# attention0: head pairs on the two row halves of TensorE, stacks through DRAM, projections and layer norms in pieces

## Chip, cores and metric

The program runs on one core of one Trainium2 chip. Its time is the device time of one execution in microseconds. A core has TensorE (PE, matmuls; PEld its weight loads), VectorE (DVE), ScalarE (ACT), GpSimd (POOL) and SyncE (SP, which here only issues DMAs). Operands lie in SBUF, matmul results in eight PSUM banks of 128 x 512 float32.

## What is computed

Two layers over x of shape 16 x 512 x 128. In each layer the normalised x goes through an attention and, beside it, through a feed-forward part whose SiLU gates the attention's result. The change touches only the attention of the first layer, with 16 heads of width 8:

```python
Q = jax.nn.relu(x @ Wq + bq)
K = jax.nn.relu(x @ Wk + bk)
V = jax.nn.relu(x @ Wv + bv)
...
scores = jnp.einsum('bqhd,bkhd->bhqk', Qh, Kh) / np.sqrt(dh)
scores = jnp.where(key_mask[:, None, None, :] == 0, NEG, scores)
scores = jnp.where(tril[None, None, :, :] == 0, NEG, scores)
attn = jax.nn.softmax(scores, axis=-1)
attn = attn * query_mask[:, None, :, None]
out = jnp.einsum('bhqk,bkhd->bqhd', attn, Vh).reshape(B, T, U)
out = out + x
```

and then a layer norm with gamma and beta. What follows it in the kernel (times the gate, plus x, and the layer norm of the next layer) is done in the same function.

## The kernel before

The program runs one stage after the other: exact layer norm, `ffn`, `attention0`, `attention1`, `experts`. `attention0` takes the span from 386 to 1429 us. It works batch by batch (16 batches of 512 tokens), each batch in two units of 8 heads, so 32 units; two batches (four units) are one turn of the loop, with the first and the last turn written out. Each engine has its own order, written by hand; semaphores tie them together.

**Operands.** A head is only 8 wide, and float32 accuracy is wanted from bf16 matmuls. So q and k are each split into three bf16 parts (ACT writes the first, `split` on POOL the two others), and six part products are stacked on the rows of one matmul: 48 rows, a mask row and, for the second pass, three rows with the parts of the row maximum. The stacks `QS` and `KS` (four buffers each, one for a unit) are filled by SP with copies of 64 KB from SBUF to SBUF, 6 for QS and 6 for KS per unit, and one mask row (`stack`, L730; `mask_row`, L735). Because the rows used are 0 to 95 or 0 to 98, a matmul of these takes the whole height of the array, and a stack holds the 8 heads of a unit.

**Two passes.** The first pass computes the scores only for the row maximum: `max_bank` (L1082, L1084) fills a PSUM bank pair `pMax` with queries on the partitions (four query blocks of width 128 to 512, since it is causal), adds `far` (a very negative triangle) with a full 128 x 128 matmul per head, and DVE takes the maximum (`maxima`, L948). `m_split` on DVE splits the 32 maxima of a unit in three parts, `turn_m` (L1136) turns them on PE, ACT copies them to SBUF (`m_evac`) and SP puts them on rows 96 to 98 of QS (`m_rows`, L740). The second pass, `score_bank` (L1095, and `add_far`, L624 and L627), computes the scores with the keys on the partitions, the maximum already subtracted; ACT takes the exponential of each bank of 512 into `PT` (`exps`, L887, five banks for two heads, two buffers `pST`). `weigh` (L1123) multiplies by the values in float32, four heads at a time in four column strips of the array; the denominators come from a column of V. ACT copies the result (`o_evac`, L892), PE turns it back (`turn_o`, L1130), and DVE divides (`o_normal`).

**Order.** In unit u, `both` interleaves the score banks of u with the max banks of u+1 (16 of them, the first ones before anything else, done by the third pair). `turn_m(u+1)` stands in the fourth pair; then the product with the values; then unit u+1 begins with `wait_ge(m_put, ...)`. In even units the next batch is prepared: transpose of x, q and k projections, and at the end the values. SP issues, in an even unit, 12 copies for QS and 6 for KS, then `m_rows`, then 6 more. All small PE results (x, q, k, v, the turned output and maxima) go through one bank, `pM`, one after another. The layer norms (`normalise`, `normalise_x1`) and the evacuation of the values (`v_evac`, L965 to L973) stand on DVE as whole blocks at the end of a unit.

Of the kernel before, what the change touches and what calls it, by code (L numbers as in the profile page):

```python
# [629 lines left out]
def attention0(nc, NB, XN, G, KM, ident, identb, far, x, Wq, bq, Wk, bk, Wv, bv, gamma, beta, x1_d, mask_d):  # L630

# [3 lines left out]
    PARTS_Q = (0, 0, 0, 1, 1, 2)  # L642
    PARTS_K = (0, 1, 2, 0, 1, 0)
    MASK, MROW = 64, 96
    VC = DH + 1
    PER_D, PER_G = 112, 20
    STACK = 7 * 16
    with ExitStack() as c:
# [7 lines left out]
        rows = sb("rows", [P, 3, P])  # L656
        xst = sb("xn_staged", [P, TOK])
# [4 lines left out]
        QS = [sb(f"QS{i}", [P, UH, TOK], BF16) for i in range(4)]  # L662
        KS = [sb(f"KS{i}", [P, UH, TOK], BF16) for i in range(4)]
        V = [sb(f"V{i}", [P, TB, HEADS * VC + 32 - VC]) for i in range(2)]
        vtmp = sb("vtmp", [P, TB, P])
        PT = [sb(f"PT{i}", [P, 5, TOK]) for i in range(4)]
        MX = sb("max", [P, UH, TB])
        mrest = sb("mrest", [P, UH * TB])
        mp = sb("mparts", [P, 3, UH * TB], BF16)
        mT = sb("mT", [UH * TB, 3, P], BF16)  # L670
        OT = sb("OT", [P, TOK])
        den = sb("den", [P, TB, 4])
# [6 lines left out]
        pST = [ps(f"pST{i}", [P, TOK]) for i in range(2)]  # L679
# [5 lines left out]
        zeroed, ones_set, v_set = sem("k_zeroed"), sem("k_ones_set"), sem("v_set")  # L685
        q_zeroed, q_ones_set = sem("q_zeroed"), sem("q_ones_set")
# [8 lines left out]
        q_stacked, k_stacked = [sem(f"q_stacked{i}") for i in range(2)], [sem(f"k_stacked{i}") for i in range(2)]  # L695
# [8 lines left out]
        loads = 3 + 2 * 2 * DH + 3  # L704

        @block.sync
        def _(sp):
# [12 lines left out]
            sp.wait_ge(mask_made, 3)  # L720
            sp.dma_start(mask_d, part[0:NT, 1, 0, 0:P]).then_inc(mask_stored, 16)
            sp.wait_ge(mask_stored, 16)

# [4 lines left out]
            def stack(i0, half, n, S, order, stacked):  # L728
                for at, k in enumerate(order):
                    sp.dma_start(S[i0 + half][DH * at:DH * at + DH, :, :],  # L730
                                 part[64 * half:64 * half + 64, n, k, :]).then_inc(stacked[half], 16)

            def mask_row(b, i0, half):
# [3 lines left out]
            def m_rows(u, i):  # L737
                mT_in.wait(sp, u)
                for k in range(3):
                    sp.dma_start(QS[i][MROW + k:MROW + k + 1, :, :], mT[:, k, :]).then_inc(m_put, 16)  # L740

# [189 lines left out]
        def _(v):  # L931
# [83 lines left out]
            for p in range(4):  # L1015
                maxima(0, p)
# [1088 lines left out]
```

## Times and profile before

| | us |
|---|---|
| median of 3 runs | 3515.97 (3511.75 to 3518.88) |
| profiled execution, device time | 3512.28 |
| its span, first to last instruction | 3510.6 |
| attention0 in it | 386 to 1429 |
| attention1 in it | 1429 to about 2900 |
| mean granted TensorE clock, whole span | 0.935 |

The page divides the span into 40 slices of 87.8 us; attention0 fills slices 5 to 17, and attention1 the next ones up to slice 33. Digits such as PE 7, DVE 6 or 7 and ACT 4 or 5 there say that no engine is busy all the time in attention0, while in attention1 PE stands at 9. The granted clock is 1.0 at 2.4 GHz and 0.5 at 1.2 GHz; a mean between the two is a mixture in time.

### The profile page before, as it was taken

Reading aid. Unit: us, or ns where it says so; the run is one execution under the profiler, and the core shown is the slowest. Engines: PE = TensorE matmul, PEld = TensorE weight load, DVE = VectorE, ACT = ScalarE, POOL = GpSimd, SP = SyncE. Lnnn points to the kernel's source line nnn. Section 1 sums busy time; section 2 is a strip of 40 time slices with the busy share of each in tenths; the row PEclk is TensorE's granted clock in tenths of the full one; section 3 lists DMA queues with packets and bytes.
Section 4 is the critical chain, followed back from the end, with each engine's and each line's share of the span. In section 5 each row is a group of like instructions: output and inputs, shape, how many; then the busy total and the mean of one; then the engine's idle time right before and its main releaser. Section 6 shows DMA issues by size and latency. Waiting matters only on the chain. (4 is left out here: it accounts for less than half of the span.)

```text
span 3510.6 us, 66700 instructions
## 1 busy us (share of the span) xinstructions
PE 2817.1 (80%) x21313; PEld 1947.4 (55%) x21313; DVE 2341.5 (67%) x5836; ACT 1521.8 (43%) x2623; POOL 1262.9 (36%) x1384
## 2 busy tenths in 40 slices
PE   0046367777777788499999999999999987999999
PEld 0024134444444444366666666666666656888888
DVE  8978657777776777466666666666666645555555
ACT  3434234454444455254555545555555532232232
POOL 4546602121211211155555555555555550000000
PEclk9986579998989899699999999999999998999999
DMA  1000123222221312101111111111111112010100
GB/s 48 0 6 0 25 30 47 39 44 35 41 45 36 51 35 32 37 28 35 34 34 34 34 34 34 34 34 34 34 34 34 32 35 64 24 36 24 34 26 24
DMA packets 152527, 116.24 MB, mean 33 GB/s; under 512 B 35506, under 2 KB 127155, under 8 KB 152372
## 3 DMA queue, kind: packets, MB, share of 16 engines
q1 hardware_dynamic: 152372, 114.25, 14.2%
q8 instruction: 87, 1.43, 0.2%
q14 instruction: 68, 0.56, 0.1%
HBM read 60.96 MB, written 17.32 MB: 22 GB/s over the span
## 5 line engine op out<-in xcount | busy, mean ns | idle before, releaser
L1539 DVE CUSTOM_DVE_ANT_0 a_scored<-a_pMax,a_causal 128x128 bf16<-128x128 f32 (+3 forms) x1024 | 449.7, 485 | 444.0 <-PE a_pMax L1663 444.0
L948 DVE TENSOR_REDUCE a_max<-a_pMax 128x2 f32<-128x256 f32 (+3 forms) x512 | 406.8, 822 | 209.3 <-PE a_pMax L1084 198.4
L887 ACT ACTIVATE a_PT<-a_pST 128x512 f32<-128x512 f32 x640 | 370.6, 597 | 403.3 <-PE a_pST L624 268.4
L1456 ACT ACTIVATE a_PT<-a_pST 128x1024 f32<-128x1024 f32 (+1 forms) x384 | 338.8, 882 | 361.2 <-PE a_pST L1653 349.8
L1082 PE MATMUL a_pMax<-a_KS,a_QS 96*128 96x128 bf16 (+3 forms) x1024 | 283.8, 329 | 203.3 <-DMA a_QS<-a_mT 134.6
L1405 POOL TENSOR_SCALAR_AFFINE_SELECT a_PT<-a_PT 128x256 f32<-128x256 f32 x512 | 203.0, 409 | 603.5 <-ACT a_PT L1456 573.0
L1942 ACT ACTIVATE m_silu<-m_pG 128x512 f32<-128x512 f32 x256 | 153.3, 599 | 410.2 <-PE m_pG L2034 410.2
L1671 PE MATMUL a_pO<-a_PT,a_V 128*64 128x512 f32 (+3 forms) x2048 | 307.3, 443 | 0.7 <-POOL a_PT L1405 0.7
L1082 PEld LDWEIGHTS a_pMax<-a_KS,a_QS 96*128 96x128 bf16 x1024 | 106.8, 105 | 309.4 <-issue 197.9
L1095 PE MATMUL a_pST<-a_QS,a_KS 99*128 99x512 bf16 (+3 forms) x1024 | 256.8, 315 | 16.4 <-ACT a_PT L887 14.4
L2042 PEld LDWEIGHTS m_pY<-m_w,m_hT 128*128 128x128 f32 x2048 | 248.0, 191 | 9.9
L815 POOL TENSOR_TENSOR a_rest<-a_qk,a_parts 128x512 f32<-128x512 f32 x32 | 37.0, 1155 | 593.9 <-ACT a_parts L880 593.7
L1989 DVE TENSOR_TENSOR m_hT<-m_pU,m_silu 128x512 f32<-128x512 f32 x256 | 177.0, 691 | 108.9 <-PE m_pU L2034 90.6
L2042 PE MATMUL m_pY<-m_w,m_hT 128*128 128x128 f32 x2048 | 248.8, 275 | 0.0
L1423 POOL TENSOR_TENSOR a_SM<-a_PT 128x768 f32<-128x768 f32 x128 | 235.0, 1836 | 10.6
L1671 PEld LDWEIGHTS a_pO<-a_PT,a_V 128*64 128x64 f32 x2048 | 136.6, 137 | 164.5 <-issue 145.3
L1910 POOL TENSOR_TENSOR m_out<-m_silu_acc,m_y 128x512 f32<-128x512 f32 x16 | 20.3, 1270 | 561.5 <-ACT m_silu_acc L1934 561.5
L1084 PE MATMUL a_pMax<-far,identb 128*128 128x128 bf16 x1024 | 221.9, 235 | 0.0
L2002 DVE SCALAR_TENSOR_TENSOR m_acc<-m_pY,m_cw,m_acc 128x128 f32<-128x128 f32 x448 | 126.3, 344 | 126.8 <-PE m_pY L2042 126.8
L1646 PE MATMUL a_pST<-a_q_high,a_k_high 64*128 64x512 f32 (+3 forms) x1024 | 198.9, 385 | 4.0 <-ACT a_PT L1456 4.0
L1653 PE MATMUL a_pST<-a_max_rows,a_ones_rows 64*128 64x512 f32 (+3 forms) x1024 | 151.8, 333 | 50.5 <-DMA a_max_rows<-a_mT 50.5
L1663 PE MATMUL a_pMax<-a_k_high,a_q_high 64*128 64x128 f32 (+3 forms) x1024 | 166.8, 363 | 8.0 <-DVE a_max L1539 6.6
(282 smaller groups left out, 6861.7 us busy)
## 6 DMA issues: line engine op xcount, KB each, us to landing
a_rden<-inverse_sums_dram SPq DMA_DIRECT2D x256, 128.0 KB, 2.9
a_QS<-a_parts SPq DMA_DIRECT2D x192, 64.0 KB
a_KS<-a_parts SPq DMA_DIRECT2D x192, 64.0 KB
a_xn_staged<-xn SPq DMA_DIRECT2D x32, 256.0 KB, 2.4
a_max_rows<-a_mT SPq DMA_DIRECT2D x512, 2.0 KB
ln_x<-in_L_attn_x SPq DMA_DIRECT2D x8, 512.0 KB, 7.2
a_x<-in_L_attn_x SPq DMA_DIRECT2D x16, 256.0 KB, 3.0
x_dram<-a_att SPq DMA_DIRECT2D x16, 256.0 KB, 3.8
```

Of the source, the lines that this page charges most:

```text
L887: a.activation(PT[p][:, k], pST[(5 * p + k) % 2][:], ACT.Exp, scale=SCALE).then_inc(exped.sem, 1)
L948: v.tensor_reduce(MX[:, 2 * p:2 * p + 2, j], pMax[j % 2][:, :, 0:(j + 1) * P], AX.X, ALU.max, negate=True).then_inc(maxed.sem, 1)
L1082: pe.matmul(pMax[j % 2][:, hh, 0:(j + 1) * P], QS[i][0:MROW, h, j * P:(j + 1) * P], KS[i][0:MROW, h, 0:(j + 1) * P], start=True, stop=False)
L1084: mm = pe.matmul(pMax[j % 2][:, hh, j * P:(j + 1) * P], identb[:], far[:], start=False, stop=True)
L1095: pe.matmul(bank[:, at:at + TOK - kb * P], KS[i][0:MROW + 3, h, kb * P:(kb + 1) * P], QS[i][0:MROW + 3, h, kb * P:TOK], start=(at == 0), s ...
L1405: g.affine_select(out=blocks, in_=blocks, compare_op=ALU.is_ge, fill=0.0, base=0, pattern=[[0, 2], [1, P]], channel_multiplier=-1).then_in ...
L1423: step.then(g.tensor_tensor(S[:, :, P:TOK], T[:, :, P:TOK], T[:, :, AT[1]:AT[1] + TOK - P], ALU.add))
L1456: a.activation(PT[s.q % 2][:, :, k * TOK:k * TOK + w], pST[:, :, 0:w], ACT.Exp, scale=SCALE).then_inc(exped.sem, 1)
L1539: last = v.tensor_tensor_reduce(scored[:, cc, at:at + w], pMax[:, cc, at:at + w], causal[:, TOK - w:], -1.0, 3e38, ALU.add, ALU.min, MX[pa ...
L1646: pe.matmul(pST[:, cc, at:at + w], K[i][rows, keys], Q[i][rows, queries], start=(n == 0 and at == 0), stop=False)
L1671: mm = pe.matmul(pO[DH * cc:DH * cc + DH, kb * P:TOK], V[pair // 2 % 2][:, kb, head:head + DH], PT[pair % 2][:, cc, AT[kb]:AT[kb] + TOK - ...
L2042: mm = pe.matmul(pY[e % 2][:, t], HT[HC * (e % 2) + k][:, t * P:(t + 1) * P], W2[:, e, k], start=(k == 0), stop=(k == HC - 1))
```

## The change

Only `attention0` is changed (and two DRAM tensors for it are declared).

- A head pair is now a head of the first eight and the same one of the second eight. The first lies on rows 0 to 63 of the array, the second on rows 64 to 127: 48 rows of part products, a row of ones against the mask row, three rows for the maximum. QS and KS hold a whole batch each (two buffers instead of four), a unit is four head pairs.
- Max pass: three rounds per pair (`max_round`) with widths 512, 128 and 384, 256 for each half; score pass: three rounds (`score_round`) of 512, 384 and 128, 256 for each half, all in one `pST` of two banks, where the next round waits for the exponential of the one before. `far` is still added with full 128 x 128 matmuls, one per half and round. Exponentials are 1024, 1024 and 512 wide.
- The max rounds run six pairs ahead of the scores (`LEAD`), so the maxima of unit u+1 are complete after the second pair of unit u.
- SP writes the parts of q and of k to DRAM (3 DMAs each and the mask row), waits for them, and loads the stacks from there: two DMAs of 448 KB for KS and two of 384 KB for QS, for the batch after this one. PE waits for them in an even unit before the third pair (`batch_stacked`).
- q and k of the batch after next are projected in odd units; the values of the next batch in even units, in two pieces, with the bias as a one-row matmul; their ReLU and copy is one ACT instruction instead of nine of DVE.
- The product with the values and both layer norms are cut in pieces which stand between score rounds (PE) or maxima (DVE).

```diff
+    PAIRS, NS, NM, LEAD = 4, 3, 3, 6
+    AT = (0, TOK, 2 * TOK, TOK + 3 * P)
+    WIDTH = (TOK, TOK, 2 * P)
+    ROUNDS = (((0, 0),), ((0, 1), (3 * P, 3)), ((0, 2),))
+    MAXB = (((3, 0),), ((0, 0), (2, P)), ((1, 0),))
...
+        pST = ps("pST", [P, 2, TOK])
...
+            def lead(self, p, last):
+                ahead = 1 if p < 2 else 2
+                if last and self.s + ahead > 3:
+                    return None
+                return self.u + ahead, (self.s + ahead) % 4, (p + 2) % PAIRS
...
+            def put_parts(dst, n, groups, put):
+                for at, count, k, parts in groups:
+                    src = part[:, n, k:k + 1, :].to_broadcast([P, count, TOK]) if parts == 1 else part[:, n, k:k + count, :]
+                    sp.dma_start(dst[at:at + count].rearrange("a s d h t -> (s d h) a t"), src).then_inc(put, 16)
...
+            def stack(b, parity, last_score=None):
+                sp.wait_ge(q_put, PUT_Q * (b + 1))
+                sp.sem_inc(puts_seen, 1)
+                sp.wait_ge(k_put, PUT_K * (b + 1))
+                sp.sem_inc(puts_seen, 1)
+                if last_score is not None:
+                    st_ready.wait(sp, last_score)
+                for half in range(2):
+                    sp.dma_start(KS[parity][key_rows(half), :, :], ks_d[:, half].rearrange("a d h t -> a d (h t)")).then_inc(k_stacked, 16)
+                for half in range(2):
+                    sp.dma_start(QS[parity][part_rows(half), :, :], qs_d[:, half].rearrange("a d h t -> a d (h t)")).then_inc(q_stacked, 16)
...
+                    n = Unit(i, s, first, last)
+                    u, b = n.u, n.b
+                    if not n.odd:
+                        if n.values:
+                            stack(b + 1, 1 - n.parity, NS * PAIRS * u - 1)
+                        if not (last and s == 0) and not (last and s == 2):
+                            stage(b + 2)
+                        if not n.no_before:
+                            load_x(b - 1)
+                    elif not n.no_before:
+                        store_x1(b - 1, 1 - n.parity)
+                    if n.prepare:
+                        put_q(b + 2)
+                    if not n.end:
+                        m_rows(u + 1, (s + 1) % 4 // 2, (s + 1) % 2)
+                    if n.prepare:
+                        put_k(b + 2)
...
+            def exp(u, p, k):
+                if k == 0:
+                st_ready.wait(a, NS * (PAIRS * u + p) + k)
+                at, w = k * TOK, WIDTH[k]
+                a.activation(PT[p][:, :, at:at + w], pST[:, :, 0:w], ACT.Exp, scale=SCALE).then_inc(exped.sem, 1)
...
+                    exp(u, 0, 2)
+                    exp(u, 1, 0)
+                    if n.prepare:
+                        q_evac(b + 2)
+                    exp(u, 1, 1)
+                    if not n.start:
...
+                    exp(u, 3, 0)
                     o_evac(2 * u)
+                    if n.prepare:
+                        k_evac(b + 2)
+                    exp(u, 3, 1)
+                    exp(u, 3, 2)
...
+            def values(b, ts=(0, 1, 2, 3)):
+                for t in ts:
+                    into = pM[:, t * P:(t + 1) * P]
+                    pe.matmul(into, XT[:, t * P:(t + 1) * P], wv[:], start=True, stop=False)
+                    mm = pe.matmul(into, one[0:1, :], rows[0:1, 0, :], start=False, stop=True)
+                if ts[-1] == TB - 1:
+                    mm.then_inc(v_ready.sem, 1)
+
+            def max_round(u, par, pair, p, m):
+                n = NM * (PAIRS * u + p) + m
+                bank = pMax[(NM * p + m) % 2]
+                maxed.wait(pe, n - 2)
+                for k, (j, at) in enumerate(MAXB[m]):
+                    w = (j + 1) * P
+                    for half in range(2):
+                        pe.matmul(bank[:, half, at:at + w], QS[par][masked_rows(half), pair, j * P:(j + 1) * P],
+                                  KS[par][masked_rows(half), pair, 0:w], start=(k == 0), stop=False)
+                for half in range(2):
+                    mm = add_far(pe, bank[:, half], [at + j * P for j, at in MAXB[m]], identb, far)
                 mm.then_inc(max_ready.sem, 1)
...
+            def score_round(u, par, pair, p, k):
+                exped.wait(pe, NS * (PAIRS * u + p) + k - 1)
+                for at, kb in ROUNDS[k]:
+                    for half in range(2):
+                        rows = split_rows(half)
+                        pe.matmul(pST[:, half, at:at + TOK - kb * P], KS[par][rows, pair, kb * P:(kb + 1) * P],
+                                  QS[par][rows, pair, kb * P:TOK], start=(at == 0), stop=False)
+                for half in range(2):
+                    mm = add_far(pe, pST[:, half], [at for at, _ in ROUNDS[k]], far, identb)
+                mm.then_inc(st_ready.sem, 1)
...
+                    def scores(p, k):
+                        score_round(u, par, PAIRS * group + p, p, k)
+                        lead(p, k)
+
+                    def weigh_before(kbs):
+                        if not n.start:
+                            weigh(u - 1, 1, 1 - group, par if n.odd else 1 - par, kbs)
+
+                    pe.wait_ge(m_put, M_PUT * (u + 1))
+                    scores(0, 0)
+                    weigh_before((0,))
+                    scores(0, 1)
+                    weigh_before((1,) if n.prepare else (1, 2, 3))
+                    if n.prepare:
+                        o_in.wait(pe, 2 * u - 2)
+                        turn_x(b + 2)
+                    scores(0, 2)
+                    scores(1, 0)
+                    if n.prepare:
+                        weigh_before((2, 3))
+                        project(b + 2, wq, q_ready)
+                    elif not n.start:
+                        o_in.wait(pe, 2 * u - 2)
+                    if n.start:
+                        mT_in.wait(pe, 0)
+                    if n.values:
+                        values(b + 1, (0, 1))
+                    scores(1, 1)
+                    if n.values:
+                        values(b + 1, (2, 3))
+                    scores(1, 2)
+                    if not n.odd and n.lead(2, last) is not None:
+                        batch_stacked(b + 1)
+                    scores(2, 0)
+                    if n.prepare:
+                        q_in.wait(pe, b + 2)
+                    if n.values:
+                        v_in.wait(pe, b + 1)
+                    if not n.start:
                         turn_o(2 * u - 1)
...
+                    weigh(u, 0, group, par, (0,))
+                    scores(2, 1)
+                    weigh(u, 0, group, par, (1,))
+                    scores(2, 2)
+                    if not n.end:
+                        o_in.wait(pe, 2 * u - 1)
+                        turn_m(u + 1)
+                    scores(3, 0)
+                    weigh(u, 0, group, par, (2, 3))
+                    if n.prepare:
                         mT_in.wait(pe, u + 1)
-                        values(b + 1)
+                        project(b + 2, wk, k_ready)
+                    scores(3, 1)
+                    scores(3, 2)
+                    if n.prepare:
+                        k_in.wait(pe, b + 2)
+                    elif n.end:
+                        o_in.wait(pe, 2 * u - 1)
+                    else:
+                        mT_in.wait(pe, u + 1)
+                    turn_o(2 * u)
```

On PE, a pair of the middle of a unit before: scores of unit u (pST) between maxima of unit u+1 (pMax), each max matmul with its own `far`.

```order
L1082 MATMUL a0_pMax1<-a0_KS2,a0_QS2 128x256
L1084 MATMUL a0_pMax1<-far,identb 128x128
L1082 MATMUL a0_pMax1<-a0_KS2,a0_QS2 128x256
L1084 MATMUL a0_pMax1<-far,identb 128x128
L1095 MATMUL a0_pST0<-a0_QS1,a0_KS1 128x384
L1095 MATMUL a0_pST0<-a0_QS1,a0_KS1 128x128
L627 MATMUL a0_pST0<-identb,far 128x2x128
L1082 MATMUL a0_pMax0<-a0_KS2,a0_QS2 128x384
```

The same place after the change, on PE, behind the projection of q (L1150); the printed name of a stack gives no row half, "x2" are the two halves.

```order
L1150 MATMUL a0_pM<-a0_xT,a0_wq 128x512 [waits a0_xT_in]
L1178 MATMUL a0_pST<-a0_QS0,a0_KS0 128x384 [waits a0_exped]
L1178 MATMUL a0_pST<-a0_QS0,a0_KS0 128x384
L1178 MATMUL a0_pST<-a0_QS0,a0_KS0 128x128 x2
L627 MATMUL a0_pST<-identb,far 128x2x128 x2
L1167 MATMUL a0_pMax0<-a0_KS1,a0_QS1 128x128 [waits a0_maxed]
L1167 MATMUL a0_pMax0<-a0_KS1,a0_QS1 128x128
L1167 MATMUL a0_pMax0<-a0_KS1,a0_QS1 128x384 x2
L627 MATMUL a0_pMax0<-far,identb 128x2x128 x2
L1178 MATMUL a0_pST<-a0_QS0,a0_KS0 128x256 [waits a0_exped]
```

What moved: matmuls on row halves and full-height `far` matmuls now alternate in blocks, twice for each score and max round, and every score round carries a wait for the exponential of the one before.

On SP, a turn before, from the preparation of a batch to the rows of the maxima.

```order
L730 DMA a_QS<-a_parts 8x8x512 [waits a0_st_ready,a0_q_parts]
L730 DMA a_QS<-a_parts 8x8x512 x11
L730 DMA a_KS<-a_parts 8x8x512 [waits a0_k_parts]
L730 DMA a_KS<-a_parts 8x8x512 x5
L735 DMA a_KS<-mask_dram 1x8x512
L740 DMA a_QS<-a_mT 1x32x128 [waits a0_mT_in]
```

And on SP after the change, from the end of an odd unit into the even one.

```order
L746 DMA k_parts_dram<-a_parts 128x3x512 [waits a0_k_parts]
L746 DMA k_parts_dram<-a_parts 128x2x512
L746 DMA k_parts_dram<-a_parts 128x512
L760 DMA k_parts_dram<-mask_dram 2x8x512
L770 DMA a_KS<-k_parts_dram 56x1x4096 [waits a0_q_put,a0_k_put,a0_st_ready]
L770 DMA a_KS<-k_parts_dram 56x1x4096
L772 DMA a_QS<-q_parts_dram 48x1x4096 x2
L741 DMA a_xn_staged<-xn 128x512 [waits a0_x_turned]
```

What moved: 24 copies of 64 KB within SBUF became 7 writes to DRAM and 4 loads from it, and the loads stand behind a wait for the writes.

## Rows read from the trace of the kernel before

**Rows 1.** Windows, the steady stretch: us, busy by engine (x instructions), PEclk, DMA share, GB/s
```profile
520.00:1400.00 880.00, 676.31 (x5839) 392.13 (x5835) 645.56 (x1655) 425.13 (x751) 171.62 (x144) 0.91 0.25 41
```

**Rows 2.** Who waited for whom in that stretch: us in total, times, longest
```profile
PE a_pMax L1082 <- DMA a_QS<-a_mT: 124.3, 29, 8.4
```

**Rows 3.** PE: one transpose group per unit; a row of the timeline, first and last start
```profile
482.01 0.33 PE L1136 MATMUL a_pM<-identb,a_mparts 128*32 128x128 bf16 x3 [0.34 <-DVEq L960]
...
L1136 PE MATMUL a_pM<-identb,a_mparts x96: 216/219/314, 451.4 to 1386.7; 128*32 128x128 bf16 x96
```

**Rows 4.** Timeline of PE, start us and length us, attention0 at an undisturbed place
```profile
1292.88 0.38 PE L1095 MATMUL a_pST<-a_QS,a_KS 99*128 99x512 bf16 x1
1293.10 0.22 PE L624 MATMUL a_pST<-identb,far 128*128 128x128 bf16 x1
1293.16 0.33 PE L1082 MATMUL a_pMax<-a_KS,a_QS 96*128 96x384 bf16 x1
...
1298.09 0.60 PE L1130 MATMUL a_pM<-ident,a_OT 128*128 128x128 f32 x4
1298.53 0.22 PE L1082 MATMUL a_pMax<-a_KS,a_QS 96*128 96x128 bf16 x1
```

**Rows 5.** Timeline of PE around one product with the values
```profile
1290.24 2.36 PE L1123 MATMUL a_pO<-a_PT,a_V 128*32 128x512 f32 x32
1292.53 0.28 PE L1082 MATMUL a_pMax<-a_KS,a_QS 96*128 96x256 bf16 x1
```

**Rows 6.** Timeline of PE in attention1: row-half pairs and their neighbours
```profile
1727.06 0.28 PE L1701 MATMUL a_pD<-a_wvT_high,a_xT_low 128*128 128x256 f32 x1
1727.27 0.50 PE L1646 MATMUL a_pST<-a_q_high,a_k_high 64*128 64x512 f32 x2
1727.61 0.39 PE L1646 MATMUL a_pST<-a_q_low,a_k_high 64*128 64x512 f32 x2
...
1728.07 0.40 PE L1653 MATMUL a_pST<-a_max_rows,a_ones_rows 64*128 64x512 f32 x2
1728.30 0.45 PE L1663 MATMUL a_pMax<-a_k_high,a_q_high 64*128 64x128 f32 x4
1728.68 2.38 PE L1671 MATMUL a_pO<-a_PT,a_V 128*64 128x512 f32 x16
```

**Rows 7.** Timeline of ACT in attention1, the two widths of exp
```profile
1724.67 0.60 ACT L1456 ACTIVATE a_PT<-a_pST 128x512 f32<-128x512 f32 x1
...
1728.51 1.02 ACT L1456 ACTIVATE a_PT<-a_pST 128x1024 f32<-128x1024 f32 x1 [0.55 <-PE a_pST L1653]
```

**Rows 8.** Groups by form in 520 to 1400: xcount, busy us, mean ns, idle before
```profile
L971 DVE TENSOR_SCALAR a_V<-a_vtmp,key_mask 128x128 f32<-128x128 f32 x56 | 58.4, 1042 | 8.3 <-DVE a_V L973 2.8 <-DVE a_vtmp L965 2.5
...
L892 ACT COPY a_OT<-a_pO 128x512 f32<-128x512 f32 x60 | 35.1, 585 | 84.4 <-PE a_pO L1123 84.4
L815 POOL TENSOR_TENSOR a_rest<-a_qk,a_parts 128x512 f32<-128x512 f32 x28 | 32.4, 1156 | 547.3 <-ACT a_parts L880 547.3
...
L880 ACT ACTIVATE a_parts<-a_pM,a_bqk 128x512 bf16<-128x512 f32 x28 | 19.3, 689 | 0.0
```

**Rows 9.** Timeline of SP: twelve of the stack copies
```profile
1321.44 7.88 SPq L730 DMA_DIRECT2D a_QS<-a_parts  x12
```

**Rows 10.** Windows: after a long wait; stack copies; the experts' weight loads
```profile
1284.00:1290.00 6.00, 6.00 (x36) 4.16 (x37) 3.69 (x10) 2.01 (x4) 0.08 (x1) 0.59 0.33 64
1322.00:1330.00 8.00, 6.29 (x51) 3.88 (x50) 7.42 (x13) 5.17 (x10) 3.42 (x3) 1.00 0.48 69
2904.00:2916.00 12.00, 0.00 (x0) 0.00 (x0) 10.85 (x18) 3.39 (x3) 0.18 (x6) 0.50 0.95 290
```

**Rows 11.** DMA issues of the run: xcount, KB each, median us to landing
```profile
x_dram<-a_att SPq DMA_DIRECT2D x16, 256.0 KB, 3.8
...
a_QS<-a_mT SPq DMA_DIRECT2D x96, 8.0 KB, 2.6
```

**Rows 12.** Timeline of PE: the first instruction of the main loop
```profile
462.56 0.27 PE L1082 MATMUL a_pMax<-a_KS,a_QS 96*128 96x128 bf16 x1 [10.66 <-DMA a_KS<-mask_dram]
```

More of the change, by code:

```diff
@@ L726, in stage @@
                 sp.dma_start(xst[:].rearrange("p (t d) -> p t d", t=TB), XN[:, bass.ds(b * TB, TB), :]).then_inc(staged, 16)
[L728 to L733, printed above, removed]
-                row = mask_d[bass.ds(b * TB, TB), :].rearrange("(o a t) p -> o a (t p)", o=1, a=1)
-                sp.dma_start(KS[i0 + half][MASK:MASK + 1, :, :], row.to_broadcast([1, UH, TOK])).then_inc(k_stacked[half], 16)
@@ L842, in residual @@
                 g.sem_inc(x1_made.sem, 1)
+            step = Steps(g, pool)
+            for b in range(2):
+                split(step, b, 0, q_in, q_parts)
+                split(step, b, 1, k_in, k_parts)
+            before = step.n
+            tail = [None]
             def turn(i, first, last):
@@ L1024, in turn @@
                 if not first:
[L1025 removed]
+                    step.base = step.base - FIRST_LESS_D
                 for s in range(4):
[L1027 to L1033 removed]
@@ L1045, in turn, with lead @@
-                    if s % 2 == 0 and not (last and s == 2):
-                        v_evac(step, b + 1, 1 - par)
-                    if s % 2 == 1 and not (first and s == 1):
-                        normalise_x1(step, b - 1, 1 - par)
+                    n = Unit(i, s, first, last)
+                    u, b = n.u, n.b
+                    before_a = (b, 0, n.parity) if n.odd else (b - 1, 1, 1 - n.parity)
+                    def lead(p, m):
+                        target = n.lead(p, last)
+                        if target is not None:
+                            maxima(target[0], target[2], m)
@@ new lines, in layer_norm @@
+                    def layer_norm(piece, odd):
+                        if n.odd == odd and not n.no_before:
+                            (normalise_x1 if odd else normalise)(step, b - 1, 1 - n.parity, piece)
+                    lead(0, 0)
+                    if not n.start:
+                        o_normal(step, 2 * u - 2, before_a[0], before_a[1], 0, before_a[2])
+                    lead(0, 1)
+                    lead(0, 2)
+                    layer_norm(0, True)
+                    lead(1, 0)
@@ L1201, in next_m @@
-                    def next_m():
-                        if more:
-                            if first and s == 0:
-                                k_in.wait(pe, b + 1)
-                            else:
-                                o_in.wait(pe, 2 * u - 1)
-                            turn_m(u + 1)
-                    pe.wait_ge(m_put, 48 * (u + 1))
-                    both(u, 0, s, range(0, 5) if more else [], i1, {0: o_first, 3: next_q})
-                    if not (first and s == 0):
-                        weigh(u - 1, 1, 1 - half, par if half else 1 - par)
```

560 lines of the change are left out of this document (263 added, 297 removed).

## The prediction

> **What bounds the kernel now.** I first read the windows of attention0's steady stretch [rows 1]: in 880 us PE is busy for 676, DVE for 646, ACT for 425, and the granted clock is 0.91. No engine is full; a chain of waits sets the pace. The table of waits [rows 2] names it: PE stands 124 us, 29 times, for the DMA that puts the rows of the maxima into QS (up to 8.4 us). The transposes of the maxima come once per unit; from the second, at 482.0, to the last, at 1386.7, there are 30 units [rows 3]: 30.16 us a unit, 60.3 us a batch. At the full clock PE streams one column per cycle: 512 columns take 0.22 us, a far matmul of 128 columns 0.06 [rows 4]. A unit's two passes are 2 x (8 heads x 1280 + 4096 columns for far) = 28672 columns, 12 us. One product with the values takes 2.29 us [rows 5], two per unit. With turns and projections that is 20 us of 30; the rest is waits and time at 1.2 GHz. After a long wait PE works at the lower level: clock 0.59 at 1284 to 1290 [rows 10].
>
> **Part 1, row halves.** In attention1 two 64-row matmuls of 512 columns, one per half, start every 0.23 us: 1727.61 to 1728.07 is two such pairs [rows 6]. So a pair runs side by side. A round of head pairs then costs 0.23 (512), 0.24 (384 and 128) or 0.12 (256), plus far on both halves, 2 x 0.06, 2 x 0.11 or 2 x 0.06. Both passes: 4 pairs x 2 x (0.35 + 0.46 + 0.24) = 8.4 us a unit against 12: a gain of 3.6.
>
> **Part 2, changing the tiling.** Far stays at full height, so each score round and each max round goes from halves to full and back. The price of one change, from attention1: full to halves, 1727.06 to 1727.27 where 256 columns need 0.12, is 0.09, and the first pair then takes 0.34 instead of 0.23; halves to full, 1728.30 to 1728.68 where 0.23 is needed, is 0.15 [rows 6]. Between 0.09 and 0.20; I take 0.13, since bf16 weights load faster than those rows' float32. Two changes per round, 24 rounds: 6.2 us a unit. That is more than part 1 gives, unless it lies in waits for ACT. "TensorEngine Tiling (Array Packing)" in the Trainium skill, Key Properties, says that a change of tiling mode drains TensorE; the gaps of 0.09 to 0.15 agree with it, and by it the gain of packing alone would be negative here.
>
> **Part 3, scores and exponentials alternate.** With a single pST a round is: score matmuls S, 0.2 us until ACT starts (last pair 1728.07 + 0.23, exp at 1728.51 [rows 6, 7]), exp 1.02, 1.02 or 0.60 [rows 7], 0.05 back. S with its changes is 0.61, 0.72, 0.50. In the cover of 1.27, 1.27 and 0.85 us PE does the max round (again 0.61, 0.72, 0.50). Bare, a pair takes 1.88 + 1.99 + 1.35 = 5.22 us and a unit 20.9.
> What else PE has to do counts only where max round and extra exceed the cover. Extras, with float32 at 1.79 ns a column (2.29 us for 1280 [rows 5]): the product with the values in pieces of 512, 384 and 384 columns, 1.0, 0.8 and 0.8 with about 0.1 for the change (1.4 where the last two stand together); a projection 0.9; a turn of four transposes 0.44 [rows 4], 0.5 with its change; half of the values 1.35, bias and changes included. Even unit, excess per round in order: 0.34 (max round 0.61 + piece 1.0 - cover 1.27), 0.85, 0, 0.69, 0.80, 0.10, 0.84, 0.25, 0, 0.14, 0, 0.20 = 4.2. Odd unit: 0.34, 0.80, 0.10, 1.04, 0.65, 0, 0.84, 0.25, 0.10, 1.04, 0.65, 0.20 = 6.0; each 0.10 is an exp behind a copy of 0.59 on ACT, each 0.65 one behind two writes of q or k of 0.69 [rows 8]. So 25.1 + 26.9 = **52.0 us a batch** from rounds alone, 8 us under today's. ACT stays below it: 10.6 us of exp and some 3.5 of copies a unit.
>
> **Part 4, DVE.** The values' evacuation leaves it: 58.4 us in 14 batches for the four main instructions alone [rows 8], about 5 us a batch. What remains, (646 - 77)/29 = 19.6 us a unit plus one more small instruction per output, fits in 26. Cutting the layer norms costs nothing on DVE and hides between maxima; if DVE fell behind, PE would wait at the max rounds, which are two rounds deep.
>
> **Part 5, the rows of the maxima.** turn_m now stands in the third pair; m_evac, two DMAs (issue 0.6 each, landing 2.6 [rows 11]) end about 5.1 us later, the unit has 6.5 left. So the 124 us go [rows 2]. Late next is the stack of the next batch.
>
> **Part 6, stacks through DRAM.** The chain starts when the k projection of an odd unit ends: 0.2 + two ACT writes 1.4 [rows 8] + split 3 x 1.16 = 3.5 on POOL [rows 8] + 0.2 + put. The put is three issues of about 0.6 us (twelve took 7.88 [rows 9]) and the mask row, and must land before the loads: a 256 KB store to DRAM lands 3.8 us after its issue [rows 11]; I take 4.5 in all. The loads: 0.6 to start, 1.70 MB, 1.5 to land. The data lie between two rows [rows 10]: weights at 290 GB/s with the DMA engines 0.95 busy, 5.9 us; SBUF copies at 69 GB/s with them 0.48 busy, 24.7 us. The low rate has its eight partitions as target, 56 or 48 now; but its share says that about half of the engines worked. Half of the engines at the rate of the weights, 290/0.95/2 = 153 GB/s, is my value: 11.2 us. Chain: 0.2 + 1.4 + 3.5 + 0.2 + 4.5 + 2.1 + 11.2 = 23.1. PE has 4.2 us of rounds left in the odd unit and 13.3 before batch_stacked: 17.5. **PE waits 5.6 us** a batch. SP holds behind those waits only the next staging and x, neither due. A shorter wait than the 8 of today, but still followed by a stretch at 1.2 GHz; in it exps hide much of PE's slowness: 1.5 us (bounds 0 and 3.5, the latter if PE alone set that stretch).
>
> **Part 7, the start.** Two batches are projected and put ahead, against fewer memsets; today the loop starts at 462.6 after a 10.7 us wait for the second half's stack [rows 12]. With the put, the first maxima come about 3 us later (436), last 13.3 + 6.6 us on DVE, and the loop starts near 456: 6 us earlier, between -5 and +12.
>
> **Sum.** 52.0 + 5.6 + 1.5 = 59.1 us a batch against 60.3: 1.2 x 15 = 18 us, plus 6, is 24. The profiled execution (3512.3, span 3510.6) would be 3488; it lies 4 us under the median, so I predict 3516 - 24 = 3492, say 3490.
>
> **Rivals.**
> (a) *The stack is hidden.* At the weights' rate the chain is 17.8 us against 17.5. Then no wait and almost no 1.2 GHz: 52.5 a batch, 7.8 x 15 + 6 = 123 us, **3393**. For it: the loads run over 56 or 48 partitions with 8 KB rows. Against: the share of 0.48 when few partitions were the target.
> (b) *Seven and six engines, slower.* If the number of engines that share a copy follows its outer counts, as 8 partitions and a share of 0.48 suggest, a KS load (7 groups of 8 rows) has 7 engines and a QS load (6 groups) 6. At 290/0.95/16 = 19.1 GB/s each, every load takes 3.4 us, 13.7 in all; PE waits 8.1 and pays 2.5 for the clock: 62.6 a batch, +2.3 x 15 - 6 = 28, **3544**. It turns to slower from 12.5 us of data on. In the Trainium skill, "DMA: Bandwidth & Descriptors", section on why a DMA increments its semaphore by 16, says just this: the largest number up to 16 that divides both outer dimensions. The share of 0.48 with 8 partitions agrees; no row has 7 or 6.
> (c) *A change of tiling costs 0.2.* 3.4 us more of PE a unit, of which some 2.3 are not covered: 56.6 a batch, wait 4.1, clock 1.5: 62.2, +1.9 x 15 - 6 = 22, **3538**. The fp32 rows speak for it, faster bf16 loads against.
> (d) *It does not do what it says*: pairs of 49-row bf16 matmuls run one after the other. 4 us more a unit, about 3600. The 64-row pairs speak against it.
>
> **How the numbers follow.** Chances: forecast 0.42 (its own range 3445 to 3525), (a) 0.25, (b) 0.17, (c) 0.11, (d) and others 0.05. About 0.2%, 7 us, is what a measurement can tell from no change. Of the forecast's 0.42, 0.34 lies under 3509, 0.05 within, 0.03 over; (a) adds 0.25 to faster, (b) and (c) 0.25 to slower and 0.03 to the same, (d) and others 0.04 to slower and 0.01 to faster. That makes 0.60, 0.08, 0.32. The range 3385 to 3555 takes in (a), (b) and (c) and leaves out (d) and a stack near 69 GB/s.
>
> **What would show it.** Right: PE waits once per batch, for a load of QS or KS, at the third pair of even units, 4 to 7 us; no wait for the maxima's rows; a unit of about 29.5 us; gaps of about 0.13 us where far follows a pair; DVE near 20 us a unit. Wrong: a DMA wait of zero (a) or above 7 (b); score rounds longer than 1.9 us without extras (c); a period of 0.45 us for a pair of 512 (d); PE waiting for DVE in max rounds, which no term holds.

## The result, and the profile after it

The changed kernel takes **3663.5 us** (3657.8 to 3667.1) against 3516.7 us in the same runs: 1.042 times as long, 95% interval 1.040 to 1.044. The prediction, 3490, and its whole range were wrong.

The windows of 520 to 1400 of the changed kernel, with the columns of [rows 1]: PE 626 us busy instead of 676, DVE 515 instead of 646, ACT 344 instead of 425, and a granted clock of 0.84 instead of 0.91. Every engine does less, and the stretch gets less far.

```profile
520.00:1400.00 880.00, 626.15 (x5003) 248.16 (x4995) 515.00 (x1384) 343.58 (x457) 151.48 (x127) 0.84 0.21 60
```

PE's waits from 600 to 1400 (us in total, times, longest), to be read against [rows 2]. The 124 us for the rows of the maxima are gone. In their place stands the stack, 12 times, 12.3 us each.

```profile
PE a_pST L1178 <- DMA a_QS<-q_parts_dram: 147.5, 12, 13.9
PE a_pST L1178 <- ACT a_PT L925: 39.4, 82, 1.1
PE a_pMax L1167 <- DVE a_max L991: 28.9, 33, 2.0
PE a_pM L1145 <- DVE a_att L1017: 13.0, 11, 1.2
```

The products with the values mark each layer's attention from its first to its last: first before, then after.

```profile
L1123 PE MATMUL a_pO<-a_PT,a_V x2048: 272/432/618, 483.0 to 1410.3; 128*32 128x512 f32 x48, 128*32 128x128 f32 x47, 128*32 128x384 f32 x46, 128*32 128x256 f32 x46
L1671 PE MATMUL a_pO<-a_PT,a_V x2048: 272/486/1061, 1488.7 to 2884.4; 128*64 128x512 f32 x48, 128*64 128x128 f32 x47, 128*64 128x256 f32 x46, 128*64 128x384 f32 x46
```

```profile
L1192 PE MATMUL a_pO<-a_PT,a_V x2048: 272/486/1063, 478.8 to 1526.5; 128*32 128x512 f32 x48, 128*32 128x128 f32 x47, 128*32 128x384 f32 x46, 128*32 128x256 f32 x46
L1759 PE MATMUL a_pO<-a_PT,a_V x2048: 272/486/1117, 1605.5 to 3036.4; 128*64 128x512 f32 x48, 128*64 128x128 f32 x47, 128*64 128x256 f32 x46, 128*64 128x384 f32 x46
```

Attention0 went from 927.3 to 1047.7 us, +120. Attention1, in which no line was changed, went from 1395.7 to 1430.9, +35. The same two lengths from the traces of all runs; each is of one profiled execution, whose time lies up to 11 us from the median in the second column:

| kernel | time | attention0 | attention1 |
|---|---|---|---|
| before | 3516.7 | 927.3 | 1395.7 |
| after | 3663.5 | 1047.7 | 1430.9 |
| e1 loads as 56 and 48 rows | 3590.9 | 974.2 | 1431.8 |
| e2 loads of an eighth | 3475.9 | 871.0 | 1437.1 |
| e3 after, DVE code shifted | 3632.9 | 1059.4 | 1399.2 |
| e4 before, DVE code shifted | 3548.0 | 930.2 | 1426.3 |
| e5 loads cut by heads | 3555.9 | 942.2 | 1442.8 |
| e6 e2 without far | 3429.0 | 823.7 | 1433.7 |
| e7 other loads later | 3651.5 | 1029.2 | 1436.4 |
| e8 e1 + e3 + e5 + e7 | 3496.2 | 913.1 | 1402.5 |
| e9 e8, PE code shifted | 3490.9 | 906.6 | 1400.1 |
| e10 e8 with filler | 3496.6 | 913.2 | 1396.1 |
| e11 e9, q projected last | **3454.9** | 873.8 | 1403.9 |

### The profile page after: what moved, and what is told of

It is laid out like the page before. It is cut to its first block and busy times, and to the rows that moved or that the text cites. A ratio compares the mean times of both kernels' runs of the same rounds, so it can differ in the third digit from the quotient of the medians.

```text
span 3662.2 us, 65148 instructions
## 1 busy us (share of the span) xinstructions
PE 2902.0 (79%) x21249; PEld 1841.6 (50%) x21249; DVE 2258.3 (62%) x5750; ACT 1493.4 (41%) x2383; POOL 1243.2 (34%) x1379
## 5 line engine op out<-in xcount | busy, mean ns | idle before, releaser
L991 DVE TENSOR_REDUCE a_max<-a_pMax 128x2 f32<-128x1024 f32 (+3 forms) x512 | 405.5, 821 | 439.2 <-PE a_pMax L624 290.6
L925 ACT ACTIVATE a_PT<-a_pST 128x1024 f32<-128x1024 f32 (+1 forms) x384 | 338.7, 882 | 500.1 <-PE a_pST L624 335.1
L1544 ACT ACTIVATE a_PT<-a_pST 128x1024 f32<-128x1024 f32 (+1 forms) x384 | 339.2, 883 | 380.5 <-PE a_pST L1741 369.4
L1178 PE MATMUL a_pST<-a_QS,a_KS 64*128 64x512 bf16 (+3 forms) x1024 | 146.8, 326 | 228.8 <-DMA a_QS<-q_parts_dram 169.3
L1759 PE MATMUL a_pO<-a_PT,a_V 128*64 128x512 f32 (+3 forms) x2048 | 321.7, 459 | 0.7 <-POOL a_PT L1493 0.7
L1178 PEld LDWEIGHTS a_pST<-a_QS,a_KS 64*128 64x128 bf16 x1024 | 39.9, 95 | 396.1 <-issue 158.0
L1511 POOL TENSOR_TENSOR a_SM<-a_PT 128x768 f32<-128x768 f32 x128 | 235.3, 1838 | 10.7
L858 POOL TENSOR_TENSOR a_att<-a_att,a_rows 128x512 f32<-128x512 f32 x16 | 20.2, 1266 | 619.8 <-DVE a_att L1052 619.8
L1192 PE MATMUL a_pO<-a_PT,a_V 128*32 128x512 f32 (+3 forms) x2048 | 202.4, 503 | 0.2 <-ACT a_PT L925 0.2
L1167 PE MATMUL a_pMax<-a_KS,a_QS 49*128 49x512 bf16 (+3 forms) x1024 | 149.6, 331 | 48.6 <-DVE a_max L991 38.4
```

Source lines behind the costliest of these rows:

```text
L925: a.activation(PT[p][:, :, at:at + w], pST[:, :, 0:w], ACT.Exp, scale=SCALE).then_inc(exped.sem, 1)
L991: last = v.tensor_reduce(MX[:, :, p, j], pMax[(NM * p + m) % 2][:, :, at:at + (j + 1) * P], AX.X, ALU.max, negate=True)
L1178: pe.matmul(pST[:, half, at:at + TOK - kb * P], KS[par][rows, pair, kb * P:(kb + 1) * P], QS[par][rows, pair, kb * P:TOK], start=(at == 0) ...
L1192: mm = pe.matmul(pO[32 * cc:32 * cc + 32, kb * P:TOK], V[par][:, kb, VC * h:VC * h + 32], PT[p][:, half, AT[kb]:AT[kb] + TOK - kb * P], st ...
L1511: step.then(g.tensor_tensor(S[:, :, P:TOK], T[:, :, P:TOK], T[:, :, AT[1]:AT[1] + TOK - P], ALU.add))
L1544: a.activation(PT[s.q % 2][:, :, k * TOK:k * TOK + w], pST[:, :, 0:w], ACT.Exp, scale=SCALE).then_inc(exped.sem, 1)
```

## The stack: one transfer in the changed kernel

SP's timeline around one stack, and the PE instruction that waited for it:

```profile
1205.37 1.56 SPq L746 DMA_DIRECT2D k_parts_dram<-a_parts  x3
1207.12 0.66 SPq L760 DMA_DIRECT2D k_parts_dram<-mask_dram  x1
1209.72 1.64 SPq L770 DMA_DIRECT2D a_KS<-k_parts_dram  x2
1211.40 1.44 SPq L772 DMA_DIRECT2D a_QS<-q_parts_dram  x2
1212.99 0.57 SPq L741 DMA_DIRECT2D a_xn_staged<-xn  x1
```

```profile
1230.20 0.61 PE L1178 MATMUL a_pST<-a_QS,a_KS 64*128 64x512 bf16 x2 [13.91 <-DMA a_QS<-q_parts_dram]
```

Put and landing take 4.35 us (forecast 4.5). From the first load's issue to PE it is 20.5 us (forecast 13.3). Windows: first this kernel while PE stands, then e7, whose loads run alone. The DMA engines are 0.40 and 0.41 busy, 6.5 of 16, at 116 and 111 GB/s.

```profile
1219.00:1227.00 8.00, 0.00 (x0) 0.00 (x0) 0.00 (x0) 0.00 (x0) 0.00 (x0) 0.50 0.40 116
```

```profile
1142.00:1154.00 12.00, 2.41 (x17) 1.41 (x15) 2.73 (x7) 2.05 (x4) 0.00 (x0) 0.74 0.41 111
```

## Experiments on the stack

**e1: the DRAM layout half by half.**

```diff
-    sp.dma_start(dst[at:at + count].rearrange("a s d h t -> (s d h) a t"), src)
+    for half in range(2):
+        sp.dma_start(dst[half, at:at + count].rearrange("a d h t -> (d h) a t"), src[split_rows(half)])
...
-    sp.dma_start(KS[parity][key_rows(half), :, :], ks_d[:, half].rearrange("a d h t -> a d (h t)"))
+    sp.dma_start(KS[parity][key_rows(half), :, :], ks_d[half].rearrange("a d h t -> (a d) (h t)"))
```

> The two part tensors in DRAM are laid out half by half, so that a load of KS is one block of 56 rows of 8 KB and a load of QS one of 48 rows; the writes become two per group of parts (SP issues 5 more DMAs per batch). Bytes and order are the same. Theory (few DMA engines work on each stack load: in the trace of the changed kernel their busy share is 0.4 at 115 GB/s while PE waits): with 14 or 16 engines at the same 18 to 19 GB/s each, 1.7 MB and the two 256 KB loads behind them take 8 us instead of 18, PE's wait for the stack falls from 12.3 us a batch to 2 to 4, a turn of two batches from 139 to about 120 us, the time from 3663 to 3500 to 3540. Rival (the loads are held by their number of bytes or by their target partitions, not by how they are cut): wait and time stay, 3650 to 3675.

3590.9 us, 1.022 (1.019 to 1.024) of before: 73 us less than the changed kernel. During the loads the engines are now 0.97 busy, at 211 GB/s:

```profile
1164.00:1173.00 9.00, 4.80 (x22) 2.65 (x18) 2.73 (x7) 2.52 (x4) 0.00 (x0) 0.50 0.97 211
```

PE's wait for the stack from 720 to 1280:

```profile
PE a_pST L1179 <- DMA a_QS<-q_parts_dram: 61.8, 9, 7.7
```

Same bytes, same rows in SBUF, other outer counts (56 and 48 instead of 7 and 6): the cut decides how many engines work. "DMA: Bandwidth & Descriptors" in the Trainium skill, section on why a DMA increments its semaphore by 16, has the rule (the largest number up to 16 that divides both outer dimensions: 7, 6, 14, 16); the busy shares of 0.40 and 0.97 agree. The time lies between theory (3500 to 3540) and rival: 6.9 us of wait a batch stayed. Two things in the trace speak for why: the rate was 211 GB/s, 13 to 14 GB/s an engine and not the 18 to 19 that I had set, and the put with its landing, now of more issues, takes 6.5 us (1155.58 to 1162.06) instead of 4.35.

**e2: almost no stack data.**

```diff
-    sp.dma_start(KS[parity][key_rows(half), :, :], ks_d[:, half].rearrange("a d h t -> a d (h t)"))
+    sp.dma_start(KS[parity][key_rows(half), 0, :], ks_d[:, half, :, 0])
```

> The stack loads bring only the first of eight heads (1/8 of the bytes), so scores of the other heads are computed on constants; all instructions of the engines stay. Theory (the wait for the stack, with the slow clock after it, is what the forecast mis-sized in attention0): the wait goes to zero, and a batch costs the 52 to 53 us that the rounds were forecast at, so a turn of two batches takes 104 to 107 us and the time is 3660 - 15.5 x 16.5 = about 3400 to 3425. Rival (the rounds themselves cost more than forecast: maxima waiting for DVE, changes of tiling, the clock): a turn still takes 112 us or more, time 3460 or more.

3475.9 us (two runs, 3467 and 3485). The wait is gone; a turn of two batches (from one jump back of PE's loop to the next) takes 112.7 us instead of 139. So the stack costs 26.3 / 2 = **13.1 us a batch**. Time and turn are the rival's: 56.3 us a batch are more than 52 to 53. The next section shows of what.

**e7: the loads of x and xn_staged after the rows of the maxima.**

> The changed kernel, with the two other loads of a batch (xn_staged and x, 256 KB each) issued after the rows of the maxima of the same unit, that is after the stack has arrived, instead of right behind the stack loads. Theory (they share the engines that carry the stack, and their 0.5 MB stands between its packets): PE's wait falls from 12.3 to 7.5 to 9.5 us a batch, the time from 3663 to 3600 to 3625. Rival (they run on other engines, or behind the stack): no change, 3655 to 3670; or a loss, if x or xn_staged comes too late for POOL and PE.

3651.5 us, 12 less, where 38 to 63 were expected; the wait is 10.7 instead of 12.3 us.

```profile
PE a_pST L1179 <- DMA a_QS<-q_parts_dram: 85.2, 8, 13.2
```

Sharing costs under 2 us. The stack's 1.70 MB alone need 18.6 us from issue (1138.17) to PE (1156.77): it is the cut, not the neighbours.

**e5: the heads of the first unit first.** SP also waits, before it writes q or k, until the last stack has landed, and PE's loop gets a second wait for the stack.

```diff
+    for group in range(2):
+        heads = slice(PAIRS * group, PAIRS * (group + 1))
...
+        sp.dma_start(KS[parity][key_rows(half), heads, :], ks_d[:, half, :, heads]...).then_inc(k_stacked[group], 16)
```

> The changed kernel with each stack load cut in two by heads: the first unit's heads 0 to 3 of KS and QS are loaded first (0.85 MB), PE waits for them alone at the old place, and for heads 4 to 7 one unit later. Same bytes, same DRAM layout, four more DMA issues per batch. Theory (the wait is the time that the loads' data take, and half of them is not needed yet): the first half is there some 9 us earlier, the wait falls from 12.3 to 3 to 5 us a batch, the time to 3525 to 3560. Rival (the wait hangs on a fixed part of the chain, on the writes and their landing, or the queue mixes both halves so that the first ends hardly sooner): 3620 to 3665.

3555.9 us, 1.011 (1.009 to 1.013) of before: as expected, 108 less than the changed kernel, without touching the layout.

**e8: all of it.**

> All together: layout half by half with the loads over 14 and 16 engines (e1), loads cut by heads (e5), the two other loads later (e7), 72 memsets ahead of attention1's loop (e3). Theory: no wait for the stack is left, a turn of attention0 takes 113 us as with the narrowed loads, attention1 1397 us: time 3440 to 3460, under the kernel before. Rival (PE still waits 2 to 4 us per batch, because writes, their landing and the first half already take longer than the time at hand): 3475 to 3510.

3496.2 us, 0.994 (0.992 to 0.996) of before: under it, but turns took 117 to 125 us, and the time is the rival's. Two waits stand in PE's table for 720 to 1280. The first is 1.8 us a batch, a little under what the rival said. The second ("issue": nothing in the profile ends it) comes at PE's jump back of the loop and was in neither. It stands in e5 too (16.7 us, 4 times), and not in the changed kernel's table:

```profile
PE a_pST L1186 <- DMA a_QS<-q_parts_dram: 16.3, 5, 4.3
PE a_pST L1186 <- issue: 16.1, 4, 4.2
```

**e11: k before q, on top of e9.** K is projected at the second pair and q at the fourth; SP issues the first KS loads before it waits for q's write.

> Kernel e9 with k projected before q: k at the second pair and q at the fourth, so that the write of k (7 issues with the mask row) leaves the end of the chain, and the first loads of KS are issued before SP waits for the write of q to land. Theory (what is left of PE's wait for the stack, 18 us in 560, and the turns of 116 to 121 us against 112.7 without the loads, are the end of the chain: 7 issues of 0.65 us, landing, loads): the chain ends 2 to 3 us earlier, the wait is nearly zero, a turn takes 113 to 116 us, time 3465 to 3480. Rival (the first load cannot start before the last score round of the old batch, and the transfer itself sets the end): within 5 us of e9, 3486 to 3496.

**3454.9 us, 0.981 (0.978 to 0.985) of before**, better than expected (3465 to 3480). Of the wait 2 us in 560 are left, attention0 (873.8) is as short as with an eighth of the data (871.0):

```profile
PE a_pST L1186 <- ACT a_PT L933: 39.8, 77, 1.1
PE a_pMax L1175 <- DVE a_max L999: 22.9, 30, 1.9
PE a_pST L1186 <- DMA a_QS<-q_parts_dram: 2.0, 2, 1.0
```

## Experiments on rounds and clock

In e2's trace at full clock, pairs and far matmuls of two rounds:

```profile
906.41 0.39 PE L1178 MATMUL a_pST<-a_QS,a_KS 64*128 64x512 bf16 x2
906.73 0.29 PE L624 MATMUL a_pST<-identb,far 128*128 128x128 bf16 x2
906.95 0.39 PE L1167 MATMUL a_pMax<-a_KS,a_QS 49*128 49x512 bf16 x2
907.27 0.29 PE L624 MATMUL a_pMax<-far,identb 128*128 128x128 bf16 x2
907.49 1.06 PE L1192 MATMUL a_pO<-a_PT,a_V 128*32 128x512 f32 x8
```

Pair to far is 0.32 where 0.22 is needed, far to the next 0.22 where 0.12 is: a change of tiling costs **0.10**, not 0.13. The pairs run side by side. The same turn and product take 0.54 and 1.0 us at 905.87 and 907.49, and 0.99 and 1.9 some 14 us later, at the unit's third pair, where the clock was at its lower level:

```profile
905.87 0.61 PE L1200 MATMUL a_pM<-ident,a_OT 128*128 128x128 f32 x4
...
920.12 1.06 PE L1200 MATMUL a_pM<-ident,a_OT 128*128 128x128 f32 x4
921.11 1.94 PE L1192 MATMUL a_pO<-a_PT,a_V 128*32 128x512 f32 x8
```

From exponential to exponential (medians of e2's turns), this place takes 4.1 to 4.2 us in three of a turn's four units, at a clock of 0.59 to 0.61, and 2.63 in the fourth, at 1.0. Two other places of the fourth unit take 5.13 and 5.57 us at 0.68 and 0.69, and 3.62 and 4.09 us at 1.0 in the second unit. So five places per turn cost 1.5 us each: 3.7 us a batch. Without them a batch is (112.7 - 7.5) / 2 = 52.6 us; this is a difference of medians, no run removed the slow time alone.

**e6: e2 without far.**

> The kernel with the narrowed stack loads (1/8 of the bytes, run e2), and without the far matmuls in attention0, which leaves out the causal mask there and with it every change between row halves and full height inside a round. Theory (far and its changes are on PE's path: by the rows 48 changes of 0.10 us and 3.7 us of far columns per unit, 8.5 us of PE's 28): a turn of two batches falls from 112.7 to 84 to 92 us, the time from 3476 to 3290 to 3350. Rival (the rounds are held by the exponentials and by the wait for the one pST, so that far is covered): a turn of 103 us or more, 3420 or more.

3429.0 us: 47 less, a turn of 108.1. The rival holds: of the 8.5 us of PE's work per unit that the expectation counts, 1.1 (by the turn) to 1.5 (by the time) came back. PE now waited 80 us for ACT from 720 to 1280 (40 in e2):

```profile
PE a_pST L1176 <- ACT a_PT L925: 80.3, 93, 1.8
```

And the granted clock (last column but two) fell from 0.92 in e2 to 0.77:

```profile
720.00:1280.00 560.00, 482.64 (x3926) 192.41 (x3924) 403.37 (x1084) 268.19 (x356) 116.40 (x98) 0.92 0.15 47
```

```profile
720.00:1280.00 560.00, 432.31 (x3103) 155.59 (x3101) 423.16 (x1161) 280.86 (x376) 117.43 (x98) 0.77 0.14 46
```

An estimate of the shares, per unit: with each busy stretch weighted by its granted clock, PE's work fell from 22.1 to 15.2 us at full clock, by 6.9 and not 8.5. Its busy time fell only from 24.3 to 20.9, and its idle time rose from 3.9 to 6.2. So of 6.9 us, 3.5 went to the lower clock, 2.3 to waits, and 1.1 came back.

**e10: e8 with the first pair of each max round issued twice.**

> Kernel e8 with each max round's first pair of matmuls issued twice (the second overwrites the first, the result is the same): 24 more pair matmuls per unit, 2.6 us of PE at full clock, in places where PE mostly waits for an exponential or a maximum right after. It tells what PE time in these rounds is worth. Theory (PE time in the max rounds is mostly covered, and the granted clock falls to half where PE does less, so that work taken away or added there comes back only in part): the granted clock in the loop rises from 0.90 or so, the unit grows by less than 1.0 us, time 3480 to 3530. Rival (PE sets the pace in the loop at a clock that does not depend on its work): a unit grows by 2.0 us or more, time 3560 or more.

3496.6 us against e8's 3496.2. The added work is smaller than the expectation says: from the first pair of a max round to its far it takes 0.54, 0.38 and 0.32 us at full clock where e8 takes 0.32, 0.32 and 0.22, so 4 x 0.38 = 1.5 us per unit and not 2.6. At full clock a unit could then not have grown by the rival's 2.0, so the run tells less than it was meant to: 1.5 us more of PE work per unit cost nothing, and the clock rose from 0.89 (e8, first line) to 0.91.

```profile
720.00:1280.00 560.00, 462.26 (x3662) 179.96 (x3660) 381.37 (x1024) 252.12 (x335) 115.60 (x97) 0.89 0.28 70
```

```profile
720.00:1280.00 560.00, 481.43 (x4093) 185.60 (x4091) 381.28 (x1017) 251.11 (x334) 115.29 (x97) 0.91 0.27 69
```

Busy time grew by 1.0 us a unit, and idle time fell by as much. Cover and clock both take part, in e6 and here; the shares are estimates from the traces, no run holds one of the two fixed.

## Experiments on the code's place

DVE in attention1, changed kernel (timeline): it stops within its own work.

```profile
2048.16 0.55 DVE L1627 CUSTOM_DVE_ANT_0 a_scored<-a_pMax,a_causal 128x384 bf16<-128x384 f32 x1
2049.99 0.08 DVE L1627 DVE_READ_ACCUMULATOR2_ANT a_max<- 128x1 f32 x1 [1.28 <-issue]
```

It does so once per batch, and then PE waits longer for the rows of the maxima (43 us from 1900 to 2800, against 31 in the kernel before), and its mean clock there is 0.99 instead of 1.00. Attention1's batches are a loop. From 1900 to 2700 the DMA queue for DVE's instructions moved 45 packets of 8 KB in the changed kernel, none in the kernel before. By a count of the two programs, DVE's loop body (266 instructions in both) starts 1548 instructions in before and 1476 after.

**e3 and e4: the same edit in the changed kernel (n = 72, start 1548) and in the kernel before (n = 184, start 1732, the place of 1476 modulo 256).**

```diff
             v.wait_ge(causal_set, 2)
+            for n_pad in range(n):
+                v.memset(pad[0:1, n_pad:n_pad + 1], 0.0)
```

> The changed kernel with 72 one-element memsets on DVE ahead of attention1's loop, in a stretch where DVE waits for PE; they shift the place of DVE's loop body of 266 instructions in its code by 72, to where it stands in the kernel before (1548 instructions in; in the changed kernel 1476). Theory (the 35 us that attention1 lost, though its code is the same, come from instruction fetches of DVE in every turn of its loop, which depend on where the body lies against the fetch blocks): DVE's pause of 1.1 to 1.7 us per batch and the fetches go, attention1 takes 1396 us instead of 1431, the time is about 3630. Rival (the pause comes from something else, such as the state of the memories or of the queues that attention0 leaves): time unchanged within 5 us, 3660 to 3668.

> The kernel before, with 184 one-element memsets on DVE at the same place, so that DVE's loop body in attention1 starts 1732 instructions in, the same place modulo 256 (and modulo 128) as in the changed kernel; the memsets take about 11 us, most of it while DVE waits for PE. Theory of the fetches: attention1 gets the pause of DVE and becomes about 35 us slower without any change in attention0, time 3545 to 3555. Rival: only what the memsets themselves cost, 3516 to 3522.

3632.9 (31 less) and 3548.0, 1.008 (1.006 to 1.011) of before: the loss goes with the place and comes with it. The waits of e4 from 1900 to 2800 and its instruction packets from 1900 to 2700 show what the changed kernel has; e3 has neither row.

```profile
DVE a_max L1542 <- issue: 10.3, 10, 1.2
```

```profile
q14 instruction: 45, 0.37, 0.2%
```

In the table above all kernels with the start at 1548, the one before among them, have an attention1 of 1396 to 1404 us, all others 1426 to 1443.

**e9: e8 with 76 short matmuls ahead of attention0's loop.**

> Kernel e8 with 76 matmuls of two columns on PE ahead of attention0's loop (some 3 us, in PE's wait for the first stack). They shift the place of PE's loop body, 1388 instructions in e8, by 152. In e5 and e8, whose body is two instructions longer than that of the changed kernel, PE pauses some 4 us at every jump back of the loop and fetches code in every turn; in the changed kernel and in e1 it does neither. Theory (whether the body stays in PE's code memory depends on the 256-instruction blocks that it touches): the pause and most of the fetches go, 6 turns x 4 us, time 3465 to 3480. Rival (the pause is a matter of length, of the two more waits, or of something else in e8): 3490 to 3502.

PE's pause and its code packets are gone from 720 to 1280 (e8's 40 in the same stretch stand below). But a turn fell only from about 121 to 119 us, and the time to 3490.9 (0.992, 0.990 to 0.994), in the rival's range and 5 us under e8, hardly more than the runs scatter: PE's waits for maxima grew from 15.5 to 25.6 us, for the stack from 16.3 to 18.1. Of the theory, that the place decides held, and the price of the fetches did not.

```profile
q8 instruction: 40, 0.66, 0.5%
```

## Why the prediction was wrong, step by step

| per batch, us | forecast | measured |
|---|---|---|
| rounds at full clock (e2) | 52.0 | 52.6 |
| time at the lower clock (e2) | 1.5 | 3.7 |
| PE's wait for the stack | 5.6 | 12.3 |
| rest of what the stack costs (13.1 - 12.3) | 0 | 0.8 |
| sum | 59.1 | 69.4 |

- **Parts 1 to 4 gave the right sum, in part by luck.** Row halves run side by side, and DVE takes 20 us a unit (403 / 20). But a change costs 0.10 and not 0.13, even units were 1.5 us shorter and odd ones 2.1 longer than summed, and the two nearly cancel. That PE waits for maxima (22.5 us in 560 in e2, 2.3 a batch) was in no term and one of the signs of being wrong; it is inside the 52.6.
- **Part 5 was right.** The wait for the rows of the maxima went.
- **Part 6 is the step that failed, by its size: 5.6 us of wait were summed and 12.3 measured.** The mechanism, PE waiting for the stack at the third pair, came as written, and put, splits and writes were right. I set 8 engines at 19.1 GB/s, 11.2 us. It was 6.5 engines at 111 to 116 GB/s, some 15 us, plus 2 us for sharing with x and xn_staged, which I had called not due. And PE had 16.0 us from the end of the k projection (1200.3) to its wait (1216.3), not 17.5. In the stack shown, the 13.9 us of wait are 8.3 more than 5.6: 5.3 for the loads alone (18.6 in e7 where 13.3 was summed), 1.9 for sharing, 1.5 for PE's earlier wait, less 0.4 before the loads. Rival (b) named the mechanism and had 0.17; even its 8.1 us were short. The rule that rival (b) cites from the Trainium skill was at hand, and one row of 0.48 with 8 partitions agreed with it; "half of the engines" was a fit to that row, not a rule.
- **The clock term was too small, and tied to the wrong cause.** The 60.3 us of before hold their share of time at 1.2 GHz; my sum of rounds replaced them with full-clock durations and kept slow time, 1.5 us, for the stack alone. What stood in the profile, 0.91 in a stretch with waits of a few us, was the warning. The interval behind the long wait takes 3.9 and 4.6 us in the changed kernel where 2.63 is the full-clock value, 1.6 a batch, as summed. But e2 has no such wait and pays as much at the same place, and 3.7 in all.
- **Part 7**: 4.2 us earlier instead of 6.
- **Attention1, +35 us, was in no term and no rival.** The 173 us between 3490 and 3663.5 are, by the two traces, 138 in attention0 (+120 where -18 was summed), 35 in attention1 and 2 at the start (the traces lie 152 us apart, the medians 147). Of the 138, 93 are Part 6: the changed kernel's attention0 is 177 us longer than e2's, and 5.6 x 15 = 84 was summed. The other 45 are in e2 as well. So Part 6 alone would have taken the time to about 3580, out of the range; this is an estimate from these traces.

## What to carry over

Look at how a DMA is cut before its bytes are counted: outer counts of 7 and 6 left more than half of the engines idle, and laying the same data out as 56 and 48 rows took back 73 of the 147 us that the change had cost. Load first what is needed first, and put the shorter write at the chain's end. A sum made of full-clock durations must not be held against a measured period that holds slow ones; and in a kernel of hardware loops, any edit can move another loop's code, so compare the stages that were not touched too.

## What the runs showed of the hardware

- A loop's cost depends on where its code lies. DVE's body of 266 instructions runs without fetches from 1548 and with 5 packets of 8 KB per turn from 1476 or 1732. PE's body of 1388 instructions (a matmul counts as two, its weight load and itself) fetches in every turn from 1825, with a pause of 4 us at the jump, and not from 1977. The changed kernel's body of 1386, from 1822, fetches nothing from 720 to 1280, but the same body at the same place has, in e3 and in e7, one turn with 9 packets and a pause of 4.4 us, so the place is not all. PE's body in the kernel before, 1493 instructions long, fetches 40 packets in 560 us too, but PE does not pause at its jump; why is open.
- "Runtime: NRT & Kernel Launch" in the Trainium skill, section on instruction fetch mechanics, says that code comes in blocks of 16 KiB, 256 instructions, and that a jump to a block not held forces a fetch. That 1476 and 1732, equal modulo 256, behave alike and 1548 does not agrees, though a smaller block would agree too; 5 packets of 8 KB do not make up whole blocks of 16 KiB.
- Less work on PE went with a lower clock: 0.92 to 0.77 for 10% less busy time (e2, e6), and 0.89 to 0.91 for 4% more (e8, e10).
- With the DMA engines 0.97 busy the stack loads, with those of x and xn_staged between them, reach 211 GB/s; the weight loads of [rows 10] reach 290 with the engines 0.95 busy. Why is open.
